# Linear attention stage of a four-layer transformer kernel: transposed key sums and outputs, an extended output matrix, an earlier norm

## The reference, cut to what matters

```python
q, k, v = phi(x @ W_q), phi(x @ W_k), x @ W_v        # phi = elu + 1, 64 wide
# scan over the tokens:
S = S + k_t[:, :, None] * v_t[:, None, :]
z = z + k_t
o_t = einsum('bij,bj->bi', S, q_t) / max(sum(z * q_t), 1e-6)
# then
x = layernorm(x + o @ W_o)
gate_logits = x @ gate_w.T                           # 16 experts
ranks = cumsum(one_hot(argmax(gate_logits)), axis=0) - 1
```

## Time and profile before

| | |
|---|---|
| median of 3 runs | 1377.04 us (1372.11 to 1378.55) |
| the profiled execution, its own time | 1373.05 us |
| its span, first to last instruction | 1371.3 us |
| mean granted TensorE clock | 0.890 |
| TensorE, VectorE, ScalarE, GpSimd busy | 79%, 61%, 47%, 27% of the span |
| linear stage | about 1065 to 1228 us of the span |

### The profile page before, as it was taken

One profiled execution on the slowest core, in us unless ns is written; L12 is line 12 of the kernel. 1 busy time (PEld: TensorE's weight loads), 2 busy tenths in 40 slices (PEclk: granted clock), 3 DMA queues, 4 the chain that ended last, 5 costly groups with the idle time before them and its releaser, 6 DMA issues. The chain is left out here.

```text
span 1371.3 us, 33015 instructions
## 1 busy us (share of the span) xinstructions
PE 1080.8 (79%) x9594; PEld 733.9 (54%) x9623; DVE 832.8 (61%) x3269; ACT 643.8 (47%) x1505; POOL 377.1 (27%) x602
## 2 busy tenths in 40 slices
PE   5989989886499994777779989998877798819950
PEld 2334444433388883676645545555566677716730
DVE  3788899985233334875645666667445677742327
ACT  2577777763344441554326656666633432204310
POOL 4012332235345444332200000000012133342554
PEclk9999999997699997999968999999999855559985
DMA  5222332312567677210032222221010011133523
GB/s 160 76 74 80 82 89 83 81 34 81 153 197 203 205 208 233 89 35 31 25 85 61 62 62 51 61 62 35 18 34 32 24 44 40 32 108 105 170 70 103
DMA packets 146579, 119.27 MB, mean 87 GB/s; under 512 B 16657, under 2 KB 134674, under 8 KB 146322
## 3 DMA queue, kind: packets, MB, share of 16 engines
q1 hardware_dynamic: 136912, 100.73, 25.8%
q0 software_dynamic: 7168, 14.37, 3.1%
q10 hardware_dynamic: 2370, 2.56, 0.7%
HBM read 47.26 MB, written 23.41 MB: 52 GB/s over the span
## 5 line engine op out<-in xcount | busy, mean ns | idle before, releaser
L655 DVE TENSOR_REDUCE mx<-pm 128x2 f32<-128x512 f32 (+1 forms) x512 | 304.8, 619 | 123.5 <-PE pm L450 74.2
L599 ACT ACTIVATE ex<-pt 128x512 f32<-128x512 f32 (+1 forms) x512 | 269.4, 547 | 163.4 <-PE pt L443 85.8
L328 POOL TENSOR_SCALAR ve<-mv 128x2 f32<-128x2 f32 x96 | 22.1, 230 | 661.3 <-DVE mv L322 660.8
L437 PE MATMUL pm<-ks,qs 64*128 64x256 bf16 (+1 forms) x1024 | 172.8, 259 | 8.3 <-DVE mx L655 5.2
L443 PE MATMUL pt<-qs,ks 64*128 64x256 bf16 (+1 forms) x1024 | 164.7, 250 | 0.6 <-ACT ex L599 0.3
L1613 POOL DMA_INDIRECT result<-ye,to_row x128 | 122.5, 957 | 151.6 <-issue 108.2
L474 PE MATMUL po<-ex,va 128*32 128x256 f32 (+1 forms) x2048 | 153.0, 371 | 6.0 <-issue 6.0
L437 PEld LDWEIGHTS pm<-ks,qs 64*128 64x128 bf16 x1024 | 74.2, 99 | 88.0 <-issue 53.4
L1536 PE MATMUL po<-he,we 128*128 128x256 f32 (+1 forms) x448 | 112.9, 395 | 0.6 <-DVE yt L1574 0.4
L424 PE MATMUL pm<-hide_q,half_id 64*128 64x256 bf16 (+1 forms) x512 | 89.1, 260 | 16.1 <-DVE mx L655 9.3
L1536 PEld LDWEIGHTS po<-he,we 128*128 128x128 f32 x448 | 85.0, 190 | 19.3 <-DVE yt L1574 0.6
(11 more groups left out here) (294 smaller groups left out, 2460.4 us busy)
## 6 DMA issues: line engine op xcount, KB each, us to landing
we<-in_pack SPq DMA_DIRECT2D x40, 514.5 KB
xs<-xg SPq DMA_DIRECT2D x96, 128.0 KB, 2.0
qs<-parts SPq DMA_DIRECT2D x192, 64.0 KB
ks<-parts SPq DMA_DIRECT2D x192, 64.0 KB
we<-in_pack SPq DMA_DIRECT2D x16, 512.0 KB
xe<-sorted SPq DMA_DIRECT2D x56, 132.0 KB, 2.2
yr<-result SPq DMA_DIRECT2D x48, 128.0 KB, 2.2
xr<-xg SPq DMA_DIRECT2D x32, 128.0 KB, 2.3
```

Source lines behind the costliest of these rows:

```text
L437: last_m = pe.matmul(mine[:, e * S + k0:e * S + k1], queries, keys[:, k0:k1], start=not causal, stop=e == 1 or not causal)
L599: nc.scalar.activation(ex[j % 2][:, :, :].rearrange("p (e g) k -> p g e k", g=2)[:, 1 - u, :, lo:S], pt[:, u, :].rearrange("p (b k) -> p b ...
L655: nc.vector.tensor_reduce(mx[q.slot % 2][:, qt, u, 2 * b:2 * b + 2], pm[:, u, :].rearrange("p (b k) -> p b k", k=S)[:, :, 0:hi], AX.X, ALU ...
```

## The change

It does the following, all of it in the linear stage of the last layer but for a buffer's shape:

- The key sums and the attention output are computed transposed (64 features by 256 tokens): the keys `tok` are now the stationary side, and `upto` or `am` the moving side, 256 and 128 columns wide. Three matmuls of 64 columns become two of 256 and 128, twice. The transposition L1042 goes.
- The output is no longer divided before its projection. Below it in one tile `zo` stands the product of key sums and queries, and `wo` gets a column of ones for it, so that the output projection also gives the denominator as a 129th column. VectorE takes its maximum and reciprocal behind the projection (`den2`, `inv3`) and multiplies while it adds the residual. `zq`, `den` and `o3` go.
- The token-side projection keeps the keys alone: `tok`, `low` and `el` are 128 columns wide where they had 256.
- The logits move from the key sums' bank to the ranks' bank, so the key sums no longer wait for `lg`; the ranks do.
- The ranks of this layer take two matmuls of 32 columns where they took five of 16. For that `seen` holds the running counts of both tiles (`run` goes).
- On VectorE, `norm_apply` moves from behind `tok` to ahead of `qt3`, and the router's parts are interleaved another way. Its waits are the same.
- At the start there are three small memsets more and one weight DMA less.

```diff
 def linear_tensor(pe, g, n, a):
-    logits, ranks = pm0[:, S:S + 2 * E3], pm1[:, S:S + 2 * E3]
+    logits, ranks = pm1[:, 0:2 * E3], pm1[:, S:S + 2 * E3]
...
         if (q := at(2)):
             s = q.slot % 2
             pe.wait_ge(am_sb, 2 * (q.n + 1))
-            wait(pe, o3_sb, q.n)
+            wait(pe, ot3_sb, q.n)
             if far(6):
                 pe.wait_ge(xrt_sb, a + far(6).n + 1)
-            k0, k1 = tok[q.slot][:, 0, 1, :], tok[q.slot][:, 1, 1, :]
-            pe.matmul(po0[:, 0:LD], am[s][:, 0, :], k0, start=True, stop=True)
-            pe.matmul(po0[:, LD:2 * LD], am[s][:, 1, :], k0, start=True, stop=False)
-            pe.matmul(po0[:, LD:2 * LD], am[s][:, 2, :], k1, start=False, stop=True).then_inc(o3_ps, 1)
+            pe.matmul(po0[0:LD, 0:S], tok[q.slot][:, 0, :], am[s][:, 0:2, :].rearrange("p a b -> p (a b)"),
+                      start=True, stop=False)
+            pe.matmul(po0[0:LD, P:S], tok[q.slot][:, 1, :], am[s][:, 2, :],
+                      start=False, stop=True).then_inc(ot3_ps, 1)
         if (q := at(1)):
             s = q.slot % 2
             pe.wait_ge(qt3_sb, q.n + 1)
             pe.wait_ge(vt3_sb, q.n + 1)
             wait(pe, am_sb, 2 * q.n)
...
             pe.wait_ge(tok_sb, q.n + 1)
             wait(pe, zq_sb, q.n)
+            pe.matmul(pm0[0:LD, 0:S], tok[q.slot][:, 0, :], upto[:, :, :].rearrange("p a b -> p (a b)"),
+                      start=True, stop=False)
+            pe.matmul(pm0[0:LD, P:S], tok[q.slot][:, 1, :], upto[:, 0, :],
+                      start=False, stop=True).then_inc(z3_ps, 1)
+        if (q := far(7)):
             if far(6):
                 pe.wait_ge(lg_sb, a + far(6).n + 1)
-            k0, k1 = tok[q.slot][:, 0, 1, :], tok[q.slot][:, 1, 1, :]
-            pe.matmul(pm0[:, 0:LD], upto[:, 0, :], k0, start=True, stop=True)
-            pe.matmul(pm0[:, LD:2 * LD], upto[:, 1, :], k0, start=True, stop=False)
-            pe.matmul(pm0[:, LD:2 * LD], upto[:, 0, :], k1, start=False, stop=True).then_inc(z3_ps, 1)
-        if (q := far(7)):
-            if far(4):
-                pe.wait_ge(res_sb, n + far(4).n + 1)
             ranks_tensor(pe, q, a, E3, ranks)
-        if (q := at(2)):
-            pe.wait_ge(o3_sb, q.n + 1)
-            wait(pe, ot3_sb, q.n)
-            wait(pe, res_sb, n + q.n)
-            pe.transpose(po1[:, 0:P], o3[q.slot % 2][:, :, :].rearrange("p t d -> p (t d)"),
-                         ident[:, :]).then_inc(ot3_ps, 1)
         if (q := far(5)):
             pe.wait_ge(ln_x, 2 * (n + q.n + 1))
             if at(2):
...
             wait(pe, xrt_sb, a + q.n)
...
                       start=True, stop=True).then_inc(t3_ps, 1)
             wait(pe, tok_sb, q.n)
             for t in range(2):
-                last = pe.matmul(pt0[:, t * P:t * P + P], xq[:, t * P:t * P + P],
-                                 wl[:, 1:3, :].rearrange("p a b -> p (a b)"), start=True, stop=True)
+                last = pe.matmul(pt0[:, t * LD:t * LD + LD], xq[:, t * P:t * P + P], wl[:, 2, :],
+                                 start=True, stop=True)
             last.then_inc(tok_ps, 1)
         if (q := at(2)):
             pe.wait_ge(ot3_sb, q.n + 1)
+            pe.wait_ge(zq_sb, q.n + 1)
             wait(pe, res_sb, n + q.n)
-            if far(7):
-                pe.wait_ge(rank_sb, a + far(7).n + 1)
             for t in range(2):
-                last = pe.matmul((pm1, po1)[t][:, t * P:t * P + P], ot3[q.slot % 2][t * LD:t * LD + LD, :],
-                                 wo[t * LD:t * LD + LD, :],
+                last = pe.matmul(po1[:, t * OW:t * OW + OW], zo[q.slot % 2][:, t * P:t * P + P], wo[:, :],
                                  start=True, stop=True)
             last.then_inc(y3_ps, 1)
         if (q := far(5)):
             pe.wait_ge(xrt_sb, a + q.n + 1)
-            if at(1):
-                pe.wait_ge(zq_sb, at(1).n + 1)
+            if far(7):
+                pe.wait_ge(rank_sb, a + far(7).n + 1)
             wait(pe, lg_sb, a + q.n)
...
-            nc.scalar.copy(ot3[q.slot % 2][:, :], po1[:, 0:P]).then_inc(ot3_sb, 1)
+            nc.scalar.copy(zo[q.slot % 2][LD:P, :], po0[0:LD, 0:S]).then_inc(ot3_sb, 1)
...
 def linear_vector(dve, n, a):
-    logits, ranks = pm0[:, S:S + 2 * E3], pm1[:, S:S + 2 * E3]
+    logits, ranks = pm1[:, 0:2 * E3], pm1[:, S:S + 2 * E3]
+    y3 = po1[:, 0:2 * OW].rearrange("p (t c) -> p t c", t=2)
...
-        routing(0, None)
-        if (q := at(2)):
-            s = q.slot % 2
-            dve.wait_ge(o3_ps, q.n + 1)
-            dve.wait_ge(den_sb, 3 * q.n + 3)
-            nc.vector.tensor_tensor(o3[s][:, :, :], po0[:, 0:2 * LD].rearrange("p (t d) -> p t d", t=2),
-                                    inv3[q.slot][:, :].unsqueeze(2).to_broadcast([P, 2, LD]),
-                                    ALU.mult).then_inc(o3_sb, 1)
-        routing(1, 0)
+        routing(0, 0)
         if (q := at(1)):
             s = q.slot % 2
             dve.wait_ge(a3_ps, q.n + 1)
+            wait(dve, y3_ps, q.back(1))
             nc.vector.tensor_tensor(am[s][:, 0:2, :], pt1[:, 0:S].rearrange("p (a b) -> p a b", a=2),
                                     upto[:, :, :], ALU.mult).then_inc(am_sb, 1)
             nc.vector.tensor_tensor(am[s][:, 2, :], pt1[:, S:S + P], upto[:, 0, :], ALU.mult).then_inc(am_sb, 1)
-        routing(2, 1)
+        routing(1, 1)
         if (q := at(1)):
             dve.wait_ge(z3_ps, q.n + 1)
-            nc.vector.tensor_tensor(zq[s][:, :, :], pm0[:, 0:2 * LD].rearrange("p (t d) -> p t d", t=2),
-                                    tok[q.slot][:, :, 0, :], ALU.mult).then_inc(zq_sb, 1)
-        routing(3, 2)
-        if (q := at(1)):
-            dve.wait_ge(zq_sb, q.n + 1)
-            nc.vector.tensor_reduce(den[s][:, :], zq[s][:, :, :], AX.X, ALU.add).then_inc(den_sb, 1)
-        routing(4, 3)
-        if (q := at(1)):
-            dve.wait_ge(den_sb, 3 * q.n + 1)
-            nc.vector.tensor_scalar(den2[s][:, :], den[s][:, :], 1e-6, None, ALU.max).then_inc(den_sb, 1)
-        routing(None, 4)
-        if (q := at(1)):
-            dve.wait_ge(den_sb, 3 * q.n + 2)
-            nc.vector.reciprocal(inv3[q.slot][:, :], den2[s][:, :]).then_inc(den_sb, 1)
-        if (q := at(0)):
-            s = q.slot % 2
-            dve.wait_ge(el_sb, 2 * q.n + 1)
-            nc.vector.scalar_tensor_tensor(qt3[s][LD:P, :], p1[LD:P, 0:S], 0.0, elt[s][LD:P, :], ALU.max,
-                                           ALU.add).then_inc(qt3_sb, 1)
-        routing(5, 5)
-        if (q := at(0)):
-            dve.wait_ge(el_sb, 2 * q.n + 2)
-            nc.vector.scalar_tensor_tensor(tok[q.slot][:, :, :, :].rearrange("p a b c -> p (a b c)"),
-                                           pt0[:, 0:S], 0.0, el[s][:, :], ALU.max, ALU.add).then_inc(tok_sb, 1)
-        routing(None, 6)
+            nc.vector.tensor_tensor(zo[s][0:LD, :], pm0[0:LD, 0:S], qt3[s][0:LD, :],
+                                    ALU.mult).then_inc(zq_sb, 1)
+        routing(2, 2)
         if (q := at(3)):
             wait(dve, xrt_ps, a + q.back(3))
             wait(dve, rows_moved[q.slot], 32 * (SEQS // SLOTS) + 16 * q.turn)
             wait(dve, scattered[q.slot], 64 * (SEQS // SLOTS) + 32 * q.turn)
             norm_apply(dve, q, n, rows=rows3[q.slot])
+        routing(3, 3)
+        if (q := at(0)):
+            s = q.slot % 2
+            dve.wait_ge(el_sb, 2 * q.n + 1)
+            nc.vector.scalar_tensor_tensor(qt3[s][0:LD, :], p1[0:LD, 0:S], 0.0, elt[s][0:LD, :], ALU.max,
+                                           ALU.add).then_inc(qt3_sb, 1)
+        routing(4, 4)
+        if (q := at(0)):
+            dve.wait_ge(el_sb, 2 * q.n + 2)
+            nc.vector.scalar_tensor_tensor(tok[q.slot][:, :, :].rearrange("p a c -> p (a c)"),
+                                           pt0[:, 0:2 * LD], 0.0, el[s][:, :], ALU.max, ALU.add).then_inc(tok_sb, 1)
+        routing(None, 5)
+        if (q := at(2)):
+            s = q.slot % 2
+            dve.wait_ge(y3_ps, q.n + 1)
+            nc.vector.tensor_scalar(den2[s][:, :, :], y3[:, :, D:OW], 1e-6, None, ALU.max).then_inc(den_sb, 1)
+        routing(5, 6)
+        if (q := at(2)):
+            dve.wait_ge(den_sb, 2 * q.n + 1)
+            nc.vector.reciprocal(inv3[q.slot][:, :, :], den2[s][:, :, :]).then_inc(den_sb, 1)
         routing(None, 7)
         if (q := at(2)):
-            dve.wait_ge(y3_ps, q.n + 1)
-            for t, bank in ((0, pm1), (1, po1)):
-                last = nc.vector.tensor_tensor(res[q.slot][:, t:t + 1, :],
-                                               bank[:, t * P:t * P + P].unsqueeze(1),
-                                               xg[:, bass.ds(2 * q.n + t, 1), :], ALU.add)
+            dve.wait_ge(den_sb, 2 * q.n + 2)
+            for t in range(2):
+                last = nc.vector.scalar_tensor_tensor(res[q.slot][:, t:t + 1, :], y3[:, t:t + 1, 0:D],
```

(32 more changed lines are left out.)

41 lines of the change are left out of this document (20 added, 21 removed).

## The result

| | before | changed |
|---|---|---|
| median | 1375.94 us (1372.11 to 1378.55, 5 runs) | 1386.46 us (1385.8 to 1389.2, 5 runs) |
| profiled execution, its own time | 1373.05 us | 1385.8 us |
| span | 1371.3 us | 1384.0 us |
| mean granted clock | 0.890 | 0.877 |

The measured ratio is 1.0099, with an interval of 1.008 to 1.0119 (the two medians of the table alone give 1.0076): the change makes the kernel about 1% slower. 1386.46 lies in the forecast range, 2.5 us under the forecast.

What follows compares the result with a forecast made beforehand. TensorE and VectorE bound the kernel before; the moved apply would make the scatter's landing bind. 13.9 + 2.2 + 1.7 - 3.4 = +14.4 on 1373.05 gives 1387.5, set at 1389 us towards the higher median; range 1378 to 1400.

Steps and rivals of the forecast that it cites:

- The step of 10.7, +13.9: Linear stage from step 8: scatter lands 6.3 us after T (end of statistics), 4.4 us follow; nine steps add 13.9.
- The start, -3.4: Linear stage up to step 7: key sums no longer wait for the logits, saving 3.4 us, bounds 0 and 7.
- The drain, +2.2 and +1.7: Steps 17 and 18 at 10.0 us each, +2.2 us; work behind step 19's apply and the last scatters, +1.7.
- landing does not decide: Rival, linear stage: scatter lands before T + 3, leaving the TensorE and VectorE loop of 8.7 us; 1366 us, chance 0.08.
- clock rises: Rival, linear stage: TensorE at full clock and no binding landing leave VectorE's 7.0 us a step; 1351 us, chance 0.02.
- TensorE's work, "about the same": TensorE's linear-stage step: wider matmuls take about the same time, 8.98 less the transposition's 0.24 giving 8.7 us, hidden.
- Two scatters apart: Rival: second scatter regularly starts 1.82 us behind the first instead of 0.30; 11 steps add 16 us, 1405, chance 0.08.

Runs made afterwards that it cites:

- b2_lg_wait: Changed kernel with the key sums waiting again for VectorE's copy of the logits; 1386.85 us, ratio 1.0099.
- a2_before_apply_ahead: Kernel before with only the apply and its waits moved ahead of the queries; 1382.91 us, ratio 1.0069.
- a1_apply_back: Changed kernel with the apply and its waits moved back to just ahead of `put` part 7; 1363.84 us, ratio 0.9914.
- a4_both: Changed kernel with the apply back behind the keys and GpSimd's scatter one step earlier, ahead of the norm arithmetic; 1346.64 us, ratio 0.9804.
- b4_both_lg_wait: a4_both with the key sums waiting again for VectorE's copy of the logits; 1353.9 us, ratio 0.9855.
- a3_scatter_early: Changed kernel with GpSimd's scatter one step earlier, ahead of the norm arithmetic, apply left ahead of the queries; 1360.19 us, ratio 0.9895.

## Why the prediction was right

*The step of 10.7, +13.9.* Right: 10.64 and +13.4. Its two parts, landing at T + 6.3 and 4.4 behind it, measured 6.02 to 6.22 and 4.50. VectorE reaches the apply after 2.0 us, not 3, so the waits are 4.1 to 4.4 each (3.7 in one step) rather than 3.3, and the list shows 53.9 us rather than 35 to 42 in the same 12 times; that changes no step, since the landing counts from T. b2_lg_wait shows it once more: 3.3 us of waiting each, the same step.

*The start, -3.4.* The size was off, and the reason is only in part shown. It was -5.8. I gave all of it to the key sums' wait and called the lighter work a possible half microsecond a step; the clock I did not count at all. Since the time up to step 3 goes between 12.1 and 15.3 in the traces of all versions, the stretch from T of step 3 to T of step 7 tells more (us, with the mean granted clock):

| | apply behind the keys | apply ahead of the queries |
|---|---|---|
| old arithmetic | 27.4 at 0.76 (before) | 24.9 at 0.84 (a2_before_apply_ahead) |
| new arithmetic | 24.3 at 0.84 (a1_apply_back), 22.1 at 1.00 (a4_both) | 21.3 at 1.00 (changed) |

Up to step 7 a1_apply_back and a4_both do the same work in the same order, and they lie 2.1 us apart with their clocks. Each figure is one profiled execution. The kernel before and the changed one differ in their clock as well:

```profile
1079.60:1107.00 27.40, 23.13 (x133) 19.95 (x133) 20.81 (x113) 11.63 (x33) 3.71 (x8) 0.76 0.09 30
1080.70:1102.00 21.30, 18.54 (x116) 14.12 (x116) 19.06 (x105) 9.84 (x33) 3.72 (x8) 1.00 0.16 51
```

At the same clock the move alone wins some 0.8 us (22.1 to 21.3), which the sum left out: with no landing to wait for, the apply fills time in which VectorE waited for the exponential (5.4 us in four waits before, 0.3 in one in the changed kernel). Restoring the key sums' wait costs 1.5 (22.7 in b2_lg_wait) to 1.9 (24.0 in b4_both_lg_wait against 22.1 in a4_both), with the clock at 0.86 in both. How much of the rest is the lighter arithmetic and how much the higher clock stays open.

*The drain, +2.2 and +1.7.* Mis-sized: +3.9 and +2.3. I took 10.0 us for each of steps 17 and 18 and left out the 1.82 us between two scatters, though the 17.9 of the kernel before contain it. It came back as 1.84 in the same step, the apply came 1.5 us late at T + 7.76, and 20.1 + 1.5 = 21.6 is what was measured, to 0.2.

*The rival "landing does not decide".* Its condition was a landing before T + 3; on the chip it was T + 6.0 to 6.2. Its price, 1366, was too high: with the condition nearly made true, a3_scatter_early gave 1360 and a4_both 1347.

*The rival "clock rises".* It was priced at 1351 with both conditions, and a4_both, which fulfils the one, got part of the other. In the changed kernel itself the clock stood at 0.50 from 1102 to 1180 us. The prediction used the 8.7 us of TensorE at the low clock as a floor below every faster case; as a figure for the low clock it holds (8.93 measured in a4_both), but the clock did not stay there, and at 1.00 the steps took 6.7. The Trainium skill's advice to keep TensorE busy for its full clock ("TensorE: Matmul & The Clock Gate", "Why this matters for your kernels") does not agree with the 10.00 of 10 us busy at 0.50, nor with a4_both, which was busy 16.00 of 16 us at 0.50 (1104 to 1120 us), while later steps kept 1.00 with 4.99 of 6.70 busy. The full step of the changed kernel is no test of it: its 32 records of matmuls took 9.20 us at 0.50 and 32 records took 4.99 at 1.00 in those steps, with 1.6 and 1.7 us idle.

*TensorE's work, "about the same".* 9.20 us busy in a full step of the changed kernel at the low clock, but with idle time between. Without any, two steps of a4_both at 0.50 lie 8.93 apart, where those of the kernel before were 8.98: about the same, as the prediction's words had it, and 0.2 over its 8.7; it had cover in either case.

*Two scatters apart.* It happened once in eleven steps, as before: no rule.

*The total.* Errors of -2.4 at the start, +1.7 and +0.6 in the drain, -0.5 in the nine steps and the 0.8 and -1.8 outside the stage cancelled to within 2 us of the forecast's +14.4: the sign and the main term are explained, and the closeness is partly luck.

## What to carry to other kernels

A wait that costs nothing where it stands has a length all the same: measure when its event comes, from the start of its own loop, before moving it. A step cannot be shorter than that time plus everything queued behind the wait on its engine, so put such a wait last in the step, or start the transfer ahead of work that doesn't feed it. And try the parts of a change apart: here the rest of the change won 0.9% together (2% with an earlier scatter), and the place of one instruction turned that into a loss of 1%.
